# Local attention inside a hybrid layer stack: the row maximum of two of four head groups moves from a matrix product into the bias of the exponential

## The reference

```python
q = _rms_norm(q); k = _rms_norm(k)
q = _apply_rotary(q, cos, sin); k = _apply_rotary(k, cos, sin)
q = q * q_gain[None, :, None, None]
mask = (pos[:, None] >= pos[None, :]) & (pos[:, None] - pos[None, :] < WINDOW)
scores = jnp.einsum('bhqd,bhkd->bhqk', q, k_full) * scale
scores = jnp.where(mask[None, None], scores, jnp.finfo(scores.dtype).min)
att = jax.nn.softmax(scores, axis=-1)
y = jnp.einsum('bhqk,bhkd->bhqd', att, v_full)
...
out = y.transpose(0, 2, 1, 3).reshape(bsz, seqlen, dim) @ Wo.T
```

## Time and profile before

| what | value |
|---|---|
| median of 3 runs | 1516.62 us (1515.74 to 1516.77) |
| the profiled execution | 1518.72 us |
| its span, first to last instruction | 1516.9 us |
| mean granted TensorE clock | 0.988 |
| busy: PE, PEld | 1443.2 us (95%), 1196.5 us (79%) |
| busy: DVE, ACT, POOL | 1046.7 us (69%), 936.7 us (62%), 809.2 us (53%) |
| local attention | from about 1042 to about 1360 us of the span |

### The profile page before, as it was taken

How to read it: one execution, slowest core, us unless ns; L and a number is a source line. 1 busy time by engine, 2 the same in 40 slices (tenths; PEclk the granted TensorE clock), 3 DMA queues, 4 the chain that set the end, 5 groups by cost and what they waited for, 6 DMA issues and landing times. The chain is left out here.

```text
span 1516.9 us, 36350 instructions
## 1 busy us (share of the span) xinstructions
PE 1443.2 (95%) x13066; PEld 1196.5 (79%) x13066; DVE 1046.7 (69%) x2272; ACT 936.7 (62%) x1760; POOL 809.2 (53%) x843
## 2 busy tenths in 40 slices
PE   4999999899998999999999999997999999989998
PEld 3777777799996788887899988886777777768886
DVE  4777877565446887785755668775777777756775
ACT  5556555465554545545655567775777777757775
POOL 2566676312013666663523257775666666636674
PEclk9999999999999999999999999999999999999999
DMA  7000000100001000000300010000000000000011
GB/s 247 2 2 2 0 2 2 35 1 1 1 1 56 2 2 0 1 2 1 125 29 15 1 40 1 0 1 2 2 1 0 0 0 0 0 2 1 31 41 42
DMA packets 21095, 26.27 MB, mean 17 GB/s; under 512 B 1904, under 2 KB 19056, under 8 KB 20848
## 3 DMA queue, kind: packets, MB, share of 16 engines
q1 hardware_dynamic: 18432, 21.64, 4.3%
q10 hardware_dynamic: 2544, 3.04, 0.6%
HBM read 20.48 MB, written 4.19 MB: 16 GB/s over the span
## 5 line engine op out<-in xcount | busy, mean ns | idle before, releaser
L543 DVE TENSOR_TENSOR ffn_h_lo<-ffn_h,ffn_h_hi 128x512 fp32r<-128x512 f32 x112 | 94.0, 841 | 116.1 <-ACT ffn_h_hi L750 116.0
L749 ACT ACTIVATE ffn_h<-ffn_hp,c_b 128x512 f32<-128x512 f32 x112 | 77.2, 689 | 153.2 <-PE ffn_hp L846 152.7
L543 DVE TENSOR_TENSOR ternary_ffn_h_lo<-ternary_ffn_h,ternary_ffn_h_hi 128x512 fp32r<-128x512 f32 x128 | 110.0, 860 | 75.0 <-ACT ternary_ffn_h_hi L750 74.8
L1187 POOL TENSOR_TENSOR ret_qk<-ret_qk,ret_qk_sin 128x512 f32<-128x512 f32 x64 | 82.6, 1291 | 103.2 <-DVE ret_qk_sin L1284 102.7
L857 PE MATMUL ternary_ffn_yp<-down_ternary,ternary_ffn_h_hi 128*128 128x256 f32 x512 | 132.6, 291 | 0.0
L857 PE MATMUL ffn_yp<-down_hi,ffn_h_hi 128*128 128x256 f32 x448 | 127.7, 285 | 0.9 <-DVE ffn_h_lo L543 0.9
L857 PE MATMUL ternary_ffn_yp<-down_ternary,ternary_ffn_h_lo 128*128 128x256 f32 x512 | 127.6, 281 | 0.0
L1193 POOL TENSOR_TENSOR ret_rstd<-ret_sums,ret_minus_half 128x16 f32<-128x16 f32 x32 | 103.7, 3240 | 42.9 <-DVE ret_sums L1326 42.9
L857 PE MATMUL ffn_yp<-down_hi,ffn_h_lo 128*128 128x256 f32 x448 | 125.2, 279 | 0.0
L857 PE MATMUL ffn_yp<-down_lo,ffn_h_hi 128*128 128x256 f32 x448 | 125.2, 279 | 0.0
L2081 POOL TENSOR_TENSOR win_rms<-win_rms,win_minus_half 128x20 f32<-128x20 f32 x31 | 115.2, 3716 | 2.6
(11 more groups left out here) (315 smaller groups left out, 4786.5 us busy)
## 6 DMA issues: line engine op xcount, KB each, us to landing
X<-in_x SPq DMA_DIRECT2D x8, 512.0 KB, 10.1
staging<-in_w SPq DMA_DIRECT2D x4, 1024.0 KB, 8.5
ffn_x_in<-in_x SPq DMA_DIRECT2D x8, 512.0 KB, 3.9
out<-X SPq DMA_DIRECT2D x7, 512.0 KB, 2.9
rotary<-in_rotary ACTq DMA_DIRECT2D x1, 1024.0 KB, 7.6
staging<-in_w_up SPq DMA_DIRECT2D x1, 1024.0 KB, 4.9
staging<-in_w_down SPq DMA_DIRECT2D x1, 1024.0 KB, 7.5
staging<-in_wqkv ACTq DMA_DIRECT2D x1, 768.0 KB, 5.9
```

The lines of the kernel that those rows point to most:

```text
L543: nc.vector.tensor_tensor(h_lo[:, m % R, :], h[:, m % R, :], h_hi[:, m % R, :].bitcast(F32), ALU.subtract).then_inc(h_ready, 1)
L749: nc.scalar.activation(h[:, m % R, :], hp[m % 2][:, :], fn, bias=bias)
L1187: nc.gpsimd.tensor_tensor(qk[:, r, :, :, :], qk[:, r, :, :, :], qk_sin[:, r, :, :, :], ALU.add).then_inc(qk_done, 1)
```

## The change

For groups 0 and 2, `lower` is left out. Instead the exponential of such a group is four instructions of 128 columns each, and each takes its block's negated row maximum as a bias, one value for each partition. Groups 1 and 3 stay as they were. The semaphore counts follow: `lowered` counts two groups for each tile and not four; ACT waits for `top_done` (the maximum) in groups 0 and 2; before it overwrites `minus_top`, DVE waits for the exponential of the tile before in these groups.

```diff
+        LOWERED = (1, 3)
...
-                at_least(dve, lowered, WKV * (n - 1) + g + 1)
+                if g in LOWERED:
+                    at_least(dve, lowered, len(LOWERED) * (n - 1) + LOWERED.index(g) + 1)
+                else:
+                    at_least(dve, exp_done, WKV * (n - 1) + g + 1)
...
             def exponential(n, g):
-                act.wait_ge(lowered, WKV * n + g + 1)
 
                 at_least(act, pt_full, WKV * (n - 1) + g + 1)
+                if g not in LOWERED:
+                    act.wait_ge(top_done, WKV * n + g + 1)
+                    for m in range(NC * PAIRS):
+                        last = nc.scalar.activation(pr[:, g, m, :], sc[:, g, m * P:(m + 1) * P], ACT.Exp,
+                                                    bias=minus_top[:, g, m:m + 1].bitcast(F32))
+                    last.then_inc(exp_done, 1)
+                    return
+                act.wait_ge(lowered, len(LOWERED) * n + LOWERED.index(g) + 1)
...
-                    if here:
+                    if here and 0 in LOWERED:
                         lower(n - 4, 0)
...
-                    if here:
+                    if here and 1 in LOWERED:
                         lower(n - 4, 1)
+                    if here and 2 in LOWERED:
                         lower(n - 4, 2)
...
-                    if here:
+                    if here and 3 in LOWERED:
                         lower(n - 4, 3)
```

## The result

The changed kernel takes 1529.78 us (median of 4 runs, 1527.98 to 1530.58) against 1516.18 us before: a ratio of 1.0086, with a 95% interval of 1.0075 to 1.0098, so 11 to 15 us more. The forecast was 1532, slower.

What follows compares the result with a forecast made beforehand. Two nearly equal paths through ACT into PE's key transpose were taken to bound the step. Longer exponentials, less slack, gave +0.51 us a step, times 30 steps 15.3 us: 1532 us, range 1524 to 1543.

Steps and rivals of the forecast that it cites:

- What bounds the kernel now: Local attention step, 9.76 us: two paths through ACT reach PE's next key transpose almost together; PE alone needs 4.11 after transpose back.
- the columns' path: ACT's gapless stream through exponentials 1 and 2 to columns_out, then PE's transpose back to the next keys; slack 0.36 us.
- Two products leave PE: PE's lower of groups 0 and 2, 0.30 and 0.21 us, together 0.5 a tile; worth it only if transpose back starts earlier.
- Eight instructions for two: ACT's exponentials of groups 0 and 2: 0.266 us a part, 1.06 a group against 0.48, so 0.58 more each.
- The bound below: ACT's parts if each bias were read under the part before: 0.70 us a group, +0.22.
- The bound above: ACT's parts if they did not overlap at all: 1.48 us a group, +1.00.
- Rival C: ACT's parts don't overlap, 0.369 us each, waiting for their own bias; step +1.3, 1556 us; chance 0.08.
- The sum for a step: Local attention, keys to keys: columns_out +0.96 us, transpose back +0.60, next keys 4.11 later; 10.24, with 0.03 added 10.27.
- From the step to the kernel: Local attention's 30 full steps at +0.51 us give 15.3 us, so the median goes from 1516.6 to 1532.
- The scale path: Square on ACT, DVE sum, POOL power, DVE pad, PE keys: 6.16 us latency; a 10.09 step, earlier and not binding.
- rival D: PE is the bound and ACT's idle 2.7 us covers the parts; step floor 9.51, -0.25, 1509 us; chance 0.06.
- the rival: The faster case: ACT, busy 191 of 264 us, hides the added 1.16 us a step; 1509 us; chance 0.06.

Runs made afterwards that it cites:

- no parts, reordered: Kernel before the change with output_high and raw_out ahead of exponential 0, columns_out ahead of exponential 2, PE's lower 0 behind project; 1511.90 us, ratio 0.9970.
- raw first: Changed kernel with output_high and raw_out moved ahead of exponential 0 on ACT; 1543.34 us, ratio 1.0172 against the kernel before the change.
- the columns first: Changed kernel with columns_out moved ahead of exponential 2 on ACT; 1525.01 us, ratio 1.0059 against the kernel before the change.
- the kernel with one piece and no bias: Changed kernel with one whole 512-column exponential in groups 0 and 2, row maximum not subtracted; 1502.67 us, ratio 0.9919 against before the change.
- the kernel of four parts without bias: Changed kernel with the bias left out of the 128-column exponentials in groups 0 and 2; 1512.74 us, ratio 0.9978 against before the change.
- the last kernel: Kernel before the change, reordered, only group 0 in four biased parts, two before and two after raw_out, square before copy; 1507.16 us, ratio 0.9946.
- group 0 alone: Kernel before the change with only group 0 in four parts with a bias, other groups keeping their product; 1521.66 us, ratio 1.0035.

## Why the prediction was right, and where its sizes were off

*What bounds the kernel now.* Two paths of nearly equal length, both through ACT: shown. Taking both away leaves 9.63, PE's own (no parts, reordered), so the waits were worth only 0.13 of the 9.76; lengthening only the columns' path costs what it is lengthened by (raw first: 10.63, 10.55 expected).

*Two products leave PE.* They are worth 0.43 us of a step if ACT pays nothing (9.63 to 9.20), where 0.5 was forecast; group 0's is 0.21 and not 0.30. In the changed kernel they are worth nothing, since PE waits for the columns. The forecast put that wait at some 0.9 us and it is 0.52. The columns come sooner than forecast, the products are worth less, and the wait for the square before the output product, which the prediction did not have, takes 0.17 of it. With the columns first, where the columns no longer hold it, PE is ready for the transpose back at 5.27 after the keys and not at the 5.09 of the kernel with one piece and no bias, for this reason. It did not enter the time of the changed kernel.

*Eight instructions for two.* The part's pitch was 0.25 and not 0.266; 1.00 for a group and not 1.06. The bound below, 0.174, by which the bias is hidden, fell with the kernel of four parts without bias: the bias's 0.095 is not hidden. The bound above, and Rival C with it, fell too: parts of 0.36 to 0.48 start 0.25 apart. The estimate of 0.294 for a part, worked out from the Trainium skill, "ScalarE: Activation LUTs", section "What ACT_TABLE_LOAD costs", was further off than the rows: the shortest part lasts 0.361 at a pitch of 0.25, where that page would give an estimated 0.387 and 0.294. The rest of its price agrees: a bias operand adds 0.095 here and about 0.093 there.

*The sum for a step*, each term with what it measured: `columns_out` starts at 5.20 (forecast 5.35), it lasts 0.71 (0.64), PE follows after 0.05 (0.14), then 4.17 to the next keys (4.11). Together 10.13 against 10.24. The mean with the loop's boundary, 10.16 against 10.27. It is the columns' path that binds, as said. Of the signs not yet named, two more held: POOL waited 3.1 us a step for the sum, where it was 2.5, and the pad in the step shown ends at 1226.99, 0.13 before the keys.

*From the step to the kernel.* 30 steps of 0.394 are 11.8 us, and 11.6 were measured from first to last keys. By the medians it is 13.6, and the interval of the ratio begins at 11.4. The two profiled executions differ by 9.3 us (1518.72, 1527.98): 11.6 in this stretch, less the 2.7 by which the one after reached the stage sooner, and 0.4 elsewhere. The one before lies 2.5 above its median and the one after 1.8 below, which gives the 13.6. That the forecast of 15.3 lies 1.7 from the medians and not the 3.5 by which its step was too long is therefore in part luck. The term that was mis-sized is the part's pitch, worth 2 x 4 x 0.016 = 0.13 us of a step; the other three (+0.07, -0.09, +0.06) nearly cancel, and the step was forecast 0.11 too long.

*The scale path.* "It is the earlier one and does not bind" held, but only by some 0.05 us. In the kernel with the columns first, whose stream on ACT is the same up to the square, this path sets the step, and it is mostly 10.07 where POOL's instruction lasts 0.59 (forecast 10.09) and 9.65 to 9.79 where it lasts 0.21. The prediction took 6.16 from one step as a latency, and that is one of two values. This did no harm to the forecast and would have spoilt its rival D, whose floor of 9.51 was 9.20 in most steps: taking the products away for nothing is worth 13 us and not 7.5.

*Where the rival went wrong.* ACT's idle time, 2.7 us a step, is real, and the last kernel uses it. The change put its parts where there was none.

What stays open: why POOL's instruction meets the rotation in some steps and not in others at the same distance of 0.04 us; and what makes the medians differ by some 2 us more than the stage does. In the other kernels the change of the median and 30 times that of the profiled step also differ, by up to 3.6 us and in either direction (group 0 alone: 6.0 against 2.5). Each step here is read from one execution; that POOL's instruction falls otherwise in others would fit, and is not shown.

## What to carry to other kernels

Splitting one instruction so that each part can take its own bias from memory costs ACT 0.095 us for each bias and about 0.05 for each further cut; price that against what it frees, here 0.21 us of PE for four parts. Before such a trade, ask in which gap of the receiving engine the new work will lie: the same four parts cost 6 us in one place of ACT's order and nothing in another. And where two latency paths end almost together, move the hand-offs of both (here columns out and the raw copy) ahead of bulk work first; with PE's `lower` 0 behind the projection, this alone gave 0.3%. Moving the raw copy alone made the changed kernel slower by another 13 us. A latency should be read from several passes of the loop: the one from the square to the keys was 6.16 us in one step and is 0.45 less in others.

## What the runs showed that was not expected

*ACT's durations grow, its pitch does not.* The parts (xcount, shortest, median and longest duration in ns) start 0.25 us apart throughout, but the longest lasts 0.115 us more than the shortest:

```profile
L2315 ACT ACTIVATE wa_probs<-wa_sc,wa_minus_top x256: 361/402/476, 1048.0 to 1361.7; 128x128 f32<-128x128 f32 x128
```

In a stretch without a gap the first group's four parts are the short ones, the second group's the long ones, and `columns_out` behind them lasts 0.71, where it was 0.63 to 0.64 before. Instructions later in such a stretch end later though they start on time, and the consumer sees the end: 0.07 us of the columns' path came from this.

*A POOL instruction over 20 columns can take 0.21, 0.39 or 0.59 us*, by what DVE does beside it. Between 0.21 and 0.59 the path to the end of the power grows by 0.45 us, in a kernel that hangs on it nearly 5% of a step.
